# A short memset behind every indirect DMA of GpSimd, and a new table for the first feed-forward's gathers

## The reference, cut to what matters

```python
x = x + 0.5 * _L0_ffn_ref(_layernorm(x), Wr, br, W1, b1, W2, b2)
x = x + _L0_attn_ref(_layernorm(x), wq, wk, wv, wproj, g_rms)
x = x + 0.5 * _L0_ffn_ref(_layernorm(x), Wr, br, W1, b1, W2, b2)

def _L0_ffn_ref(x, Wr, br, W1, b1, W2, b2):       # 8 experts, one for each token
    expert_idx = jnp.argmax(xf @ Wr.T + br, axis=-1)
    h = jax.nn.relu(jnp.einsum('td,efd->etf', xf, W1) + b1[:, None, :])
    y = jnp.einsum('etf,edf->etd', h, W2) + b2[:, None, :]
    out = y[expert_idx, jnp.arange(xf.shape[0])]
```

## Time and profile before

| | before |
|---|---|
| median of 3 runs | 532.01 us (531.59 to 533.94) |
| profiled execution, span from the first to the last instruction | 529.2 us |
| first feed-forward, from the first gather to the end of the last Ys | 32.95 to 160.00 us |
| second feed-forward, start of its first output and of its last | 424.3 to 523.2 us |
| PE busy | 85% |
| DVE busy | 73% |
| ACT busy | 66% |
| POOL busy | 56% |

### The profile page before, as it was taken

How to read it: one execution, slowest core, us unless ns; L and a number is a source line. 1 busy time by engine, 2 the same in 40 slices (tenths; PEclk the granted TensorE clock), 3 DMA queues, 4 the chain that set the end, 5 groups by cost and what they waited for, 6 DMA issues and landing times.

```text
span 529.2 us, 13928 instructions
## 1 busy us (share of the span) xinstructions
PE 447.8 (85%) x4108; PEld 329.2 (62%) x4108; DVE 385.8 (73%) x1052; ACT 348.0 (66%) x782; POOL 297.5 (56%) x439
## 2 busy tenths in 40 slices
PE   7968997886987999999999989987968788887794
PEld 4338886775764565656556555654644477776794
DVE  5876675777687698989989898867657468654572
ACT  4335664675746788989899988866556755453561
POOL 8044555686746778686865844576335244444343
PEclk9899999999896899999999999978789999898998
DMA  7942324251100000000000000000001221131100
GB/s 215 285 190 56 90 61 130 56 165 30 33 22 16 11 14 14 12 12 12 10 7 2 4 3 2 2 18 13 32 28 35 55 78 52 53 83 57 48 25 11
DMA packets 28649, 27.02 MB, mean 51 GB/s; under 512 B 5684, under 2 KB 25947, under 8 KB 28018
## 3 DMA queue, kind: packets, MB, share of 16 engines
q1 hardware_dynamic: 24034, 17.65, 11.0%
q0 software_dynamic: 4544, 8.49, 5.6%
HBM read 16.56 MB, written 12.71 MB: 55 GB/s over the span
## 4 chain that ended last, share of the span: by engine, by line
PE 39%; DVE 14%; issue 10%; ACT 7%; another core or an unknown queue 3%; POOL 1%; DVEq 1%; ACTq 1%; POOLq 0%
DVE Smax L1733 7%; PE PS L991 7%; PE PS L851 7%; PE PS L944 6%; PE PS L967 6%; PE PS L868 5%; PE PS L926 4%; ACT Pt L1205 3%; PE PS L910 2%; ACT QkT L1112 2%; PE PS L1021 2%; DVE St L1362 2%; POOL out L617 1%; DVEq L1607 1%
## 5 line engine op out<-in xcount | busy, mean ns | idle before, releaser
L1733 DVE TENSOR_REDUCE Smax<-PS 128x4 f32<-128x1024 f32 x128 | 155.9, 1224 | 46.0 <-PE PS L944 39.0
L1205 ACT ACTIVATE Pt<-PS 128x1024 f32<-128x1024 f32 x128 | 126.4, 1024 | 23.1 <-PE PS L967 19.0
L851 PE MATMUL PS<-XsT,Ws 128*128 128x128 f32 x624 | 90.2, 289 | 22.0 <-ACT XsT L1112 15.9
L1153 ACT ACTIVATE HsT<-PS,Bs 128x128 f32<-128x128 f32 x168 | 52.0, 366 | 74.7 <-PE PS L851 48.0
L851 PEld LDWEIGHTS PS<-XsT,Ws 128*128 128x128 f32 x624 | 78.0, 195 | 30.5 <-ACT XsT L1112 19.3
L868 PE MATMUL PS<-W,HsT 128*128 x624 | 87.5, 284 | 9.2 <-DVE Ys L1633 4.8
L868 PEld LDWEIGHTS PS<-W,HsT 128*128 128x128 f32 x624 | 78.1, 196 | 14.9 <-issue 14.5
L991 PE MATMUL PS<-Pt,Vg 128*32 128x256 f32 x1024 | 73.7, 409 | 0.9 <-issue 0.7
L1622 DVE TENSOR_SCALAR HsT<-PS,Bs 128x128 f32<-128x128 f32 x144 | 43.7, 345 | 41.0 <-PE PS L851 24.4
L617 POOL DMA_INDIRECT out<-AtCol x39 | 38.1, 978 | 57.6 <-DVE AtCol L1633 39.8
L597 POOL DMA_INDIRECT Pt<-rows,TokI x39 | 40.4, 1035 | 51.4 <-DVE Ys L1633 22.0
(11 more groups left out here) (227 smaller groups left out, 695.5 us busy)
## 6 DMA issues: line engine op xcount, KB each, us to landing
AtCol<-slots SPq DMA_DIRECT2D x39, 65.5 KB, 1.4
rows<-XX SPq DMA_DIRECT2D x8, 288.0 KB, 4.3
XX<-x SPq DMA_DIRECT2D x8, 256.0 KB, 4.3
W<-w1T SPq DMA_DIRECT2D x2, 1024.0 KB, 6.1
W<-w2T SPq DMA_DIRECT2D x2, 1024.0 KB, 9.1
mid<-mid_second SPq DMA_DIRECT2D x1, 1472.0 KB
mid<-Ys SPq DMA_DIRECT2D x16, 64.0 KB
QkT<-NmaxT SPq DMA_DIRECT2D x64, 4.0 KB
```

The costliest lines, as they stand in the source:

```text
L851: last = nc.tensor.matmul(PS[:, h_bank(n) + c // 2, (c % 2) * P:(c % 2 + 1) * P], Ws[:, n % R_WS, c * P:(c + 1) * P], XsT[:, n % 2, :], st ...
L1153: last = nc.scalar.activation(HsT[:, n % 2, c, :], PS[:, h_bank(n) + c // 2, (c % 2) * P:(c % 2 + 1) * P], ACT.Relu, bias=Bs[:, n % 2, c:c ...
L1205: nc.scalar.activation(Pt[:, m % 2, 2 * pair:2 * pair + 2, :, :].rearrange("p h c t -> p (h c t)"), PS[:, score_bank(m, pair):score_bank(m ...
L1733: nc.vector.tensor_reduce(Smax[:, b % 2, :, at:at + 33:32].rearrange("p t h -> p h t"), PS[:, max_bank(m, pair):max_bank(m, pair) + 2, :]. ...
```

## The change

Each of the four functions ends with a call of `pause()`: a memset of 352 fp32 elements per partition of a tensor that nothing reads, on GpSimd. It waits on the semaphore of the memset before it. The table of gathers is dealt anew: nine instead of seven ahead of the first tile; two at tiles 4, 8, 12 instead of 5 and 10; none at tiles 15 to 21 instead of 15 to 17; two at tiles 22 and 23 instead of one.

```diff
-FIRST_XS = 7
+FIRST_XS = 9
...
-GATHERS = {5: 2, 10: 2, 15: 0, 16: 0, 17: 0}
+GATHERS = {4: 2, 8: 2, 12: 2, 15: 0, 16: 0, 17: 0, 18: 0, 19: 0, 20: 0, 21: 0, 22: 2, 23: 2}
...
+PAUSE = 352
...
+        Unread = sb("Unread", [P, PAUSE])
...
+            pauses = [0]
+
+            def pause():
+
+                if pauses[0]:
+                    pool.wait_ge(paused, pauses[0])
+                nc.gpsimd.memset(Unread[:], 0.0).then_inc(paused, 1)
+                pauses[0] += 1
+
             def gather(t):
                 u = t % R_XS
                 if t >= R_XS:
...
                     bounds_check=N_TILES * P - 1, oob_is_err=False).then_inc(ring_moved[u], 16)
+                pause()
```

More of the change, by code:

```diff
@@ L331, in program @@
         const_done = sem("const_done")
+        paused = sem("paused")
         block = ctx.enter_context(nc.Block())
```

## The result

The changed kernel takes **517.44 us** (median of 4 runs, 514.62 to 519.85) and the kernel before 532.98 (4 runs on the same chip, 531.59 to 536.87): ratio **0.972**, 95% interval 0.966 to 0.978. Faster, as forecast, but 14 us of span won instead of 22: the profiled execution went from 529.2 to 515.3 us.

A forecast was written before the change was run, and what follows sets the result against it. Bound: PE's completions held by close indirect DMAs. Terms -26.0 +1.0 -2.5 +4.4 -1.0 +1.5 +0.4 +0.3 = -21.9 take the span from 529.2 to 507.3, with 2.8 more 510 us; own range 500 to 518, 8-in-10 range 499 to 529.

The forecast's parts named there:

- Reading of the bound: Whole kernel: indirect DMAs 1.28 to 1.35 us apart join their holds on PE's completions into 2 to 3 us.
- Durations: On POOL: a fill takes 0.40 us, and neighbouring indirect DMAs come to stand 1.58 us apart.
- -26.0 + 1.0: ACT's waits behind close indirect DMAs: all 26 us go, less 1.0 for chains of four or nine at 1.58.
- Half: Rival, chance 0.17: chains of three and more still hold PE at 1.58 us; half of 26 returns, 523 us.
- One sign of being wrong: Pauses of PE, DVE and ACT ending 1.8 us behind a chain's last DMA in spite of the fills.
- Tiles 0 to 21 of the first feed-forward: Sign expected in the profile after: these tiles together shorter by 8 to 10 us.
- +4.4: Tiles 22 to 25: sequence 0's second rope ends 4.4 us later, half from two extra gathers, half from fills.
- -3.3 of the holds: Attention: ACT's copy YuT waits 3.6 us behind indirect DMAs; 3.3 of it counted as hold that goes.
- -2.5: Granted clock, lower behind several pauses: 2.5 us come back, bounds 0 and 6.8.
- DVE held by fills: Rival, chance 0.07: fills hold DVE through the shared port, 22 us on the path; 532 us, no change.
- Xr at 0.7 us in most tiles: Sign of being wrong: DVE's Xr, 0.35 us alone, takes 0.7 us in most tiles.

The follow-up runs named there:

- fills where needed: Kernel before plus fills: 512 elements behind gathers 0 to 23 and placements, 352 behind others, second feed-forward's scatters only in four catch-up tiles; 516.88 us, ratio 0.978.

## Why the prediction was right, and where it was not

- **Reading of the bound: right.** The pauses of all engines with a cause called "remote" belong to indirect DMAs that follow each other closely. Shown by the same DMAs at other distances: with a fill of 0.17 us the pauses stay, with 0.41 they shrink, with 0.55 they are all but gone, and the table without fills changes nothing. Why DMAs at a short distance do this is not shown.
- **Durations: right.** Fill 0.41 us (0.40 taken); distance 1.59 between gathers and 1.54 between scatters (1.58).
- **"-26.0 + 1.0", the holds and their residue: the step that was mis-sized.** I took 1.42 us as enough because one *pair* at 1.42 was harmless, and applied it to chains. At tiles 56 and 57 a chain at 1.54 keeps (5.25 - 4.24) of (6.60 - 4.24), some 43% of its hold. In the second feed-forward alone the residue is 92.2 - 87.6 = 4.6 us, against 1.0 for the whole kernel. So it shortened by 6.7 us, where I had written 11 to 14. This is what the rival "Half" said, and the result (517.4) lies halfway between its 523 and the forecast's 510: the forecast's own range of 500 to 518 held it by 0.6 us. One sign of being wrong came true in part: at 462.61 the pause ends 1.56 us behind the last DMA of a chain, in spite of the fills.
- **Tiles 0 to 21 of the first feed-forward: wrong.** 8 to 10 us were to come; tile 21 ends at 93.13 instead of 94.59, 1.5 us. The gathers are a chain from the start, and tiles 4, 6 and 16 still take 3.15, 3.95 and 3.11 us. Up to tile 14 nothing at all was won (76.06 against 75.95). That this is the same residue is argued from the size of those tiles; the longer early fills speak for it and don't show it.
- **"+4.4", the late rope: the mechanism right, the price on the path not.** DVE waits 4.8 us, 3.8 more (5 to 7 were written). But tiles 22 to 29 take only 27.5 us instead of 25.9, +1.6; tile 27 is 3.7 longer and tile 22, whose hold went, 2.2 shorter. And it comes from the fills, not from the table.
- **Attention and clock (-3.3 of the holds, -2.5): roughly.** Attention gave 4.7 us. The eight undisturbed kernels with fills of 352 or more behind every DMA take 258.9 to 263.0 there, the four with no fills in that stage or fills of 64 take 263.2 to 267.6; "fills where needed", which has them there, takes 265.3. So there is a gain, and its size is known to several us only. Over the whole the mean granted clock went from 0.948 to 0.953, while the fills alone had 0.947 and won 2.5 us more. In the second feed-forward it rose from 0.97 to 1.00 and PE's busy time for the same matmuls fell from 82.1 to 81.0 us; in the first it fell from 0.99 to 0.97 and PE's rose from 105.7 to 107.1. So no gain by the clock is shown.
- **DVE held by fills.** Its price of 22 us was far off, its mechanism half right. Xr, 28.1 us in all before, takes 41.2, and the add of residual and bias 26.0 instead of 22.9. The price was also counted over 84 fills; with the 16 fetches of the first feed-forward it is 100. The Trainium skill (SBUF — State Buffer, "SBUF: two separate sides") made me look for a hold as long as the fill. The rows show that one and another: of the 78 Xr after the change 10 end 0.08 us behind the end of a fill, as the page would have it, and 31 end with the *DMA* that has a fill waiting behind it, before the fill has worked. The sign "Xr at 0.7 us in most tiles" thus came near (0.571 in the mean of the second feed-forward) without its price: about 0.09 us in a lone tile.

## What to carry to other kernels

When all engines stop together and the profile names no cause, look at what GpSimd issues in the 2 us before: indirect DMAs 1.3 us apart held PE's results here, and 1.67 us from start to start, kept by idle work where GpSimd has time, freed them in nearly every place. Read the safe distance from chains, not from a pair, don't lengthen the stretches in which GpSimd is behind, and sum a wait over all its labels before calling it gone. A table of issue slots that leaves the distance inside a chain alone moves nothing.

## What I had not expected of the hardware

- The hold depends steeply on the distance between indirect DMAs: 3.79, 2.96 and 0.9 us of waiting at 1.30 to 1.39, 1.54 and 1.67 us. In one place it outlasted a distance of 1.67, once begun. Why PE's completions are held at all stays open; none of these runs looks below the DMA's start and end.
- VectorE's Xr is held to the end of an indirect DMA (0.84 us instead of 0.34) when GpSimd has a ready memset of 352 elements behind that DMA, and is free when nothing is ready, or another indirect DMA (16 of 18 such took under 0.40 us before the change). Behind a ready memset of 64 elements it is nearly free too (39 of 46 take under 0.40 us). Why the length counts is not shown.
